# Cross-attention: the causal mask of two of four score banks is added by VectorE in place of a TensorE product

## The reference, cut to what matters

```python
qh = (layernorm(x) @ Wq.T)   # 16 heads of width 32
k, v = split(ctx @ Wkv_expand.T)        # of the first 100 context positions
scores = einsum('bhqd,bhkd->bhqk', qh, kh) / sqrt(32)
scores = where(tril(ones(sq, sk)), scores, finfo.min)   # causal mask
attn = softmax(scores)
x = x + einsum('bhqk,bhkd->bhqd', attn, vh) @ Wout.T
```

## Time and profile before

| | before |
|---|---|
| median of three runs | 2577.39 us (2575.33 to 2578.66) |
| the profiled execution, time | 2567.62 us |
| the profiled execution, span of the core | 2565.8 us |
| mean granted TensorE clock | 0.982 |
| busy: TensorE, VectorE, ScalarE, GpSimd | 96%, 61%, 52%, 33% |

### The profile page before, as it was taken

One profiled execution on the slowest core, in us unless ns is written; L12 is line 12 of the kernel. 1 busy time (PEld: TensorE's weight loads), 2 busy tenths in 40 slices (PEclk: granted clock), 3 DMA queues, 4 the chain that ended last, 5 costly groups with the idle time before them and its releaser, 6 DMA issues.

```text
span 2565.8 us, 47726 instructions
## 1 busy us (share of the span) xinstructions
PE 2458.2 (96%) x16474; PEld 1333.3 (52%) x16474; DVE 1553.2 (61%) x3592; ACT 1339.9 (52%) x4109; POOL 843.8 (33%) x794
## 2 busy tenths in 40 slices
PE   6998999999999999999889999999999999999998
PEld 3554555554555555444454465465465465465466
DVE  7786766666666666666555745644645645655644
ACT  4554555555555555555454554554554563564533
POOL 3333333333333333333222422422422422422412
PEclk9999999999999999999979999999999999999999
DMA  6786667777677767797611001001001001001000
GB/s 157 149 180 161 152 151 162 167 161 169 138 170 162 168 144 190 157 195 171 139 59 57 30 13 53 5 14 54 1 18 54 1 18 54 1 18 41 7 17 14
DMA packets 456281, 241.79 MB, mean 94 GB/s; under 512 B 389136, under 2 KB 391824, under 8 KB 455284
## 3 DMA queue, kind: packets, MB, share of 16 engines
q1 hardware_dynamic: 456034, 238.63, 39.8%
HBM read 78.66 MB, written 32.77 MB: 43 GB/s over the span
## 4 chain that ended last, share of the span: by engine, by line
PE 89%; DVE 4%; ACT 3%; issue 3%; POOL 1%; DVEq 0%; POOLq 0%; ACTq 0%
PE ps L1561 24%; PE ps L1562 24%; PE ps L1563 24%; PE ps L1740 3%; PE ps L1741 2%; PE ps L1742 2%; PE ps L1854 2%; ACT mem L982 2%; PE ps L1838 1%; PE ps L1810 1%; PE ps L1750 1%; PE ps L1754 1%; PE ps L1752 1%; PE ps L1832 1%; PE ps L1579 1%
## 5 line engine op out<-in xcount | busy, mean ns | idle before, releaser
L1561 PE MATMUL ps<-mem 128*128 128x512 f16 (+7 forms) x3992 | 1227.9, 326 | 47.7 <-issue 31.4
L1562 PE MATMUL ps<-mem 128*128 128x512 f16 (+7 forms) x3992 | 1239.5, 326 | 0.0
L1563 PE MATMUL ps<-mem 128*128 128x512 f16 (+7 forms) x3992 | 1223.0, 325 | 0.0
L1561 PEld LDWEIGHTS ps<-mem 128*128 128x128 f16 (+3 forms) x3992 | 413.6, 104 | 374.6 <-issue 52.8
L1563 PEld LDWEIGHTS ps<-mem 128*128 128x128 f16 (+3 forms) x3992 | 414.7, 104 | 316.5 <-issue 8.6
L1562 PEld LDWEIGHTS ps<-mem 128*128 128x128 f16 (+3 forms) x3992 | 416.4, 104 | 304.8 <-issue 8.0
L757 POOL TENSOR_TENSOR mem<-mem 128x500 f32<-128x500 f32 (+1 forms) x231 | 268.7, 1164 | 470.3 <-ACT mem L1058 289.7
L707 POOL TENSOR_TENSOR mem<-mem 128x8 f32<-128x8 f32 x100 | 163.7, 1637 | 507.4 <-DVE mem L1145 507.4
L852 ACT ACTIVATE mem<-ps,mem 100x100 f32<-100x100 f32 x512 | 169.1, 346 | 186.4 <-DVE mem L1175 185.5
L1513 DVE TENSOR_TENSOR mem<-mem 128x500 f16<-128x500 f32 (+1 forms) x231 | 144.5, 649 | 171.3 <-ACT mem L1040 167.4
L719 POOL TENSOR_TENSOR mem<-mem 100x400 f16<-100x400 f32 x128 | 158.7, 1239 | 182.7 <-ACT mem L862 182.7
(11 more groups left out here) (123 smaller groups left out, 3043.9 us busy)
## 6 DMA issues: line engine op xcount, KB each, us to landing
x<-mem SPq DMA_DIRECT2D x100, 256.0 KB, 2.8
mem<-x SPq DMA_DIRECT2D x75, 256.0 KB, 3.6
mem<-in_x SPq DMA_DIRECT2D x50, 256.0 KB, 3.5
mem<-x SPq DMA_DIRECT2D x12, 1000.0 KB
mem<-mem SPq DMA_DIRECT2D x32, 200.0 KB
mem<-mem SPq DMA_DIRECT2D x6, 1000.0 KB
out<-mem SPq DMA_DIRECT2D x6, 1000.0 KB
mem<-in_wq SPq DMA_DIRECT2D x16, 256.0 KB, 4.2
```

Source lines behind the costliest of these rows:

```text
L1561: pe.matmul(out_ap, ah, bh, start=(i == 0), stop=False)
L1562: pe.matmul(out_ap, ah, bl, start=False, stop=False)
L1563: mm = pe.matmul(out_ap, al, bh, start=False, stop=(i == len(pairs) - 1))
```

## The change

For banks 2 and 3 TensorE's product with the mask is left out; the score products overwrite instead of accumulating; and VectorE adds the mask in PSUM, in place, waits for that addition and then takes the maximum. Banks 0 and 1 stay as they were. TensorE's waits for the exponentials of all four banks stay where they are.

```diff
+        MASKED_BY_DVE = (2, 3)
...
                 def largest_scores(b, i):
                     n = g * 4 * GB + 4 * b + i
                     dve.wait_ge(c["sc"], n + 1)
+                    if i in MASKED_BY_DVE:
+                        block = ps[0:S, i, 0:HG * S].rearrange("p (h t) -> p h t", h=HG)
+                        dve.tensor_tensor(block, block, mask[0:S, :, :], ALU.add).then_inc(c["hid"], 1)
+                        dve.wait_ge(c["hid"], (g * GB + b) * len(MASKED_BY_DVE) + i - MASKED_BY_DVE[0] + 1)
                     dve.tensor_reduce(cmx[0:S, i, :],
...
-                            pe.matmul(ps[0:S, i, 0:HG * S], ident16[0:S, 0:S],
-                                      mask[0:S, :, :].rearrange("p h k -> p (h k)"),
-                                      start=True, stop=False)
+                            if i not in MASKED_BY_DVE:
+                                pe.matmul(ps[0:S, i, 0:HG * S], ident16[0:S, 0:S],
+                                          mask[0:S, :, :].rearrange("p h k -> p (h k)"),
+                                          start=True, stop=False)
...
                                                ckT[r0:r0 + CD, m, b * S:(b + 1) * S],
-                                               start=False, stop=(m == KC - 1))
+                                               start=i in MASKED_BY_DVE,
+                                               stop=i in MASKED_BY_DVE or m == KC - 1)
```

More of the change, by code:

```diff
@@ L282, in decoder_layer @@
                  "rl rexp chain spread mT mTe a am ahi alo base gb sg0 ub lora gs us sgs "
-                 "h hhi hlo ad dt dsum dhi dlo yp add moved late latehi latelo ved")
+                 "h hid hhi hlo ad dt dsum dhi dlo yp add moved late latehi latelo ved")
         c = {n: sem("c_" + n) for n in names.split()}
```

## The result

Over 20 runs each the changed kernel takes 2579.72 us (median), the kernel before 2574.78 us on the same chips: ratio 1.0024, interval 1.0017 to 1.0031. It is slower by some 4 to 8 us, just over the 0.2% named in the prediction, which had 4 us less. The profiled execution takes 2577.97 us with a span of 2576.2 us, 10.4 us more than the span shown of before.

A forecast was written before the change was run, and what follows sets the result against it. TensorE, busy for 96% of the span, was taken as the bound. Groups 1 to 5 (-1.4 us), group 0 (-1.9) and group 6 (-0.7) sum to -4.0 us, giving 2573.4 us; 8-in-10 range 2565.5 to 2579.5 us.

The forecast's parts named there:

- The price of an addition: On VectorE, each masked bank's in-place addition takes 0.574 us plus 0.04 for its wait, adding 0.61 us.
- Rival A: Addition with its wait adds only 0.49 us, copy 2 stays covered: 11.2 us gained, 2566.2 us; 0.37 with partial cases.
- B: Addition on VectorE costs 0.72 us, mix at S+5.48: +1.1 us, 2578.5 us, still no change; 0.48 together with the forecast.
- C: In-place PSUM write makes VectorE's addition or the wake-up long; passes +0.2% at 0.81 us, 2582.6 us; chance 0.10.
- D: With half its mask products gone in group 0, TensorE's clock comes back later; +0.2% would take 18 us; chance 0.05.
- group 0: Cross-attention group without projection pieces and with TensorE at low clock; forecast sum -1.9 us.
- groups 1 to 5: Cross-attention groups with forecast periods of 7.87 and 8.14 us in turn, against 7.99; -1.4 us for all five.
- Copy 2: VectorE's copy of transpose 2, which the mix waits for; forecast not covered, ending at S+5.21 instead of S+4.04.
- S: Start of an iteration's score products on TensorE in the cross-attention loop, from which times are offsets; period 7.99 us before.
- mix: TensorE's product with the values (L1810) in the cross-attention loop; forecast at S+5.26 instead of S+5.04, 0.22 us late.
- group 6: Cross-attention group with two batches, where VectorE's copies wait for TensorE; additions covered, both iterations keep all: -0.7 us.
- the end of the sum: Where each of groups 1 to 5 hands over from its loop to TensorE's own work, forecast -0.28 us per group.

The follow-up runs named there:

- new order: Changed kernel with VectorE's copy 2 ahead of the second addition, maxima 2 and 3 waiting for two semaphores: 2560.72 us; with 4 small writes 2558.29 us.
- N = 20: Kernel before with 20 small VectorE writes to idle cells at the start of VectorE's program: 2586.22 us, ratio 1.0044.
- changed kernel with 4 or 24 writes: Changed kernel with 4 or 24 small VectorE writes at the start of VectorE's program: 2561.31 us with 4, 2560.39 us with 24.

## Why the prediction was wrong

- **The price of an addition: right.** 0.573 us against the 0.574 taken from the earlier trace rows; the maximum starts 0.60 us behind the addition (1512.09 to 1512.69), forecast 0.61. Rival A's rule, the Trainium skill's (VectorE: DVE Perf Modes, "The DRAIN you can't avoid"), would have had it at the 0.49 us pitch; the trace disagrees by 0.11 us. Rivals B and C needed 0.72 and 0.81 us and fall with it. D falls too: group 0 became shorter, the clock came back earlier, and over the cross-attentions of groups 1 to 5 it is 1.00 in both kernels. The falls lie in the stages between them, which no rival looked at.
- **The mechanism inside the loop: right.** Copy 2 at S+5.20 (forecast 5.21), mix at S+5.30 (5.26; TensorE starts 0.10 us behind the copy, not 0.05), periods 7.91 and 8.11 (7.87 and 8.14). From the first mask product to the first transpose of the last iteration, in TensorE's timeline, groups 1 to 5 became shorter by 0.14, 0.16, 0.02, 0.15 and 0.16 us, 0.6 together where 1.4 was forecast (in group 1 the second scores come 0.54 us earlier and not 0.64, and each later period is 0.03 to 0.04 off); group 0 by 1.5 (1.9); group 6 by 0.7 (0.7): 2.8 us against the 4.0 of the sum. Up to its last transpose group 0 gained 2.4 us, which makes 3.7 in all. There the clock is in play: it is back at its upper level 44.3 us behind the group's first mask product (47.6 in the kernel before), but the kernel before also has 3.4 us at that level inside the group. That 3.7 comes so near to 4.0 is in part luck: the five groups were put too high, and the last 0.9 us of group 0 are no step of the forecast. The new order shows the same from the other side: with copy 2 ahead of the second addition an iteration takes 7.74 us instead of 7.99, so 0.25 of the 0.34 us are kept.
- **The step that failed** is the end of the sum, where each group "hands over to TensorE's own work" and nothing further is counted. The 20 additions ahead of the loop were costed as time on VectorE and not as 20 places in its queue, and the loop's head was taken as free. It cost 3 x (4.5 - 2.2) = 7 us by the stretches above; 7 - 3.7 is 3 us slower, and the granted clock took away 6.9 us more in the profiled execution (18.8 against 11.9), part of it in the same stretches. By the medians, 20 places alone cost 11 us (7 to 15; N = 20 against before), which holds these 7 us and whatever the clock adds; 11 less the 4 us of the gain is 7, inside the measured loss of 4 to 8 us. How much of the clock's share belongs to the stalls is not shown. At the same place of the code the change is a gain: ratio 0.9949 against 0.9977 behind the border, 1.0024 against 1.0044 on it, that is 7 and 5 us, each with some 5 us to either side; the forecast of 4 us is inside both.
- **It could have been seen.** The kernel before has three rows of 3.65 to 3.75 us on "issue" at L1465, 11.2 us in all, with TensorE waiting behind two of them. I had read rows around the change only. No rival had this place: C was slower by the addition's price and D by group 0's clock.
- **The profiled execution of before** was 10 us below its median. Its own clock and start differ from those of other executions by as much as the effects argued about: the start of the first mask product, ahead of anything changed, was 3.0 us later in the changed kernel's profile, which is no effect of the change.

What stays open: whether the new order makes the kernel faster than the changed order at the same place of the code. The traces say 4.2 us in the cross-attention, the same in all profiles; the medians (2558.29, 2559.64 and 2560.72 against 2560.39 and 2561.31 us) say 0 to 3 us, with intervals of some 4 us to either side of each. The granted clock took away 12.6, 12.7 and 17.7 us in the new order's executions without a stall and 10.2, 12.3 and 13.6 in the changed order's, so the clock may take part of it back; that is an argument and not shown. It is also not shown why the clock falls. One of the changed kernel's falls began during TensorE's wait behind a stall (1754.3 us) and one right behind such a wait (2150.3), but three others between 1400 and 2560 us (1945.5, 2140.0 and 2338.0) had no gap over 0.15 us between TensorE's products in the 12 us before them. Nor is it shown why the packet of code comes some 6.5 us behind the last instruction ahead of the jump.

The best versions (the changed kernel with 4 or 24 writes, the new order with or without its 4) are all 0.5 to 0.7% faster than the kernel before, 13 to 17 us. Some 6 us of that come from the place of the loop alone.

## What to carry to other kernels

With a hardware loop in the program, an edit ahead of it moves the loop's head in the queue of each engine that it touches, and one instruction there was worth 16 us here, four times what the edit itself was. So before the arithmetic of an edit, look in the timeline for "issue" rows behind each jump back on every engine, count how many places the edit adds ahead of the head (doubled waits too), and compare versions at the same place, or with a few idle instructions put ahead to move it. A small difference measured without that says nothing of the edit.

## What was not expected of the hardware

- VectorE's jump back costs a stall that depends on one instruction's place: 8.3 to 8.5 us (once 8.95) with the body's first vector instruction at number 2456 (or 2712), none to be seen at 2457. In all kernels that stall, the stall ends 8.3 to 8.5 us (once 8.95) after the last instruction ahead of the jump, 1.5 us (once 2.0) behind a packet of code; code of the first block never held VectorE up longer than the 2.0 to 2.7 us in which it waits for TensorE anyway.
- A second semaphore to wait for is an instruction of its own in the unrolled code: 24 in the page's count, of which the 20 ahead of the loop moved its head.
- VectorE's write in place to PSUM costs nothing more than its write to SBUF: 0.573 against 0.574 us for 400 columns.
- More is lost to the clock in the kernels with the long stalls: 17.1 to 19.8 us in the kernels with stalls of 8.4 us, 10.2 to 14.4 us in those without, but for one with 17.7. Part of the falls come with TensorE busy throughout.
